# Seeding the scores' bank with the mask: a ScalarE copy in place of a TensorE product, in a six-layer decoder stack

## The reference

```
q = l2norm(q) * qs
k = l2norm(k) * ksc
... rotary turn of q and k with scales
mask = (it < jb) | (it > jb + w) | (jb == -1)
sim = jnp.einsum('bhwie,bhwje->bhwij', bq, bk2) * QK_SCALE
sim = jnp.where(mask, -jnp.finfo(sim.dtype).max, sim)
attn = jax.nn.softmax(sim, -1)
out = jnp.einsum('bhwij,bhwje->bhwie', attn, bv2)
```

## Time and profile before

| | us |
|---|---|
| median of 3 runs | 1274.28 (1273.89 to 1277.31) |
| the profiled execution | 1272.33 |
| its span in the trace | 1270.5 |
| layers, first to last mask | 410.7 to 1220.7 |
| TensorE busy in the span | 1138.3 (90%) |
| VectorE busy | 949.0 (75%) |
| ScalarE busy | 847.5 (67%) |
| GpSimdE busy | 650.1 (51%) |

### The profile page before, as it was taken

One profiled execution on the slowest core, in us unless ns is written; L12 is line 12 of the kernel. 1 busy time (PEld: TensorE's weight loads), 2 busy tenths in 40 slices (PEclk: granted clock), 3 DMA queues, 4 the chain that ended last, 5 costly groups with the idle time before them and its releaser, 6 DMA issues. The chain is left out here.

```text
span 1270.5 us, 26317 instructions
## 1 busy us (share of the span) xinstructions
PE 1138.3 (90%) x9636; PEld 720.2 (57%) x9636; DVE 949.0 (75%) x1399; ACT 847.5 (67%) x1356; POOL 650.1 (51%) x522
## 2 busy tenths in 40 slices
PE   7787869999765899999999999999999999999976
PEld 2222337777422576666656676666666666667541
DVE  2789957777465778787878788877878787878733
ACT  4553536665335588777877788678877787777844
POOL 1555723444323675664657465655566465756510
PEclk9888979999786899999999999999999999999997
DMA  3000007110200454344525453435434453534310
GB/s 113 1 1 0 1 17 217 51 50 1 77 24 19 97 155 99 93 123 107 133 74 129 103 134 88 112 102 134 99 98 123 109 126 76 126 90 120 87 49 17
DMA packets 75510, 107.11 MB, mean 84 GB/s; under 512 B 25347, under 2 KB 31938, under 8 KB 75002
## 3 DMA queue, kind: packets, MB, share of 16 engines
q1 hardware_dynamic: 75386, 105.47, 31.9%
HBM read 30.89 MB, written 0.59 MB: 25 GB/s over the span
## 5 line engine op out<-in xcount | busy, mean ns | idle before, releaser
L1680 POOL TENSOR_TENSOR st_sq_sum<-h 128x512 f32<-128x512 f32 x96 | 123.5, 1287 | 250.0 <-ACT h L1426 249.4
L1563 DVE SCALAR_TENSOR_TENSOR st_turned<-banks,mo_w 128x1024 f32<-128x1024 f32 x96 | 117.6, 1225 | 74.6 <-ACT banks L1437 43.2
L1426 ACT ACTIVATE h<-banks 128x512 f32<-128x512 f32 x192 | 112.1, 596 | 68.2 <-PE banks L1269 64.9
L1684 POOL TENSOR_TENSOR mo_w<-mo_w,x 128x512 f32<-128x512 f32 x96 | 122.5, 1276 | 61.4 <-DVE x L1549 60.5
L1330 PEld LDWEIGHTS banks<-st_p_blocks,st_vs 128*64 128x64 f32 x1536 | 81.8, 138 | 78.6 <-issue 74.6
L1289 PEld LDWEIGHTS banks<-st_wv,stream 128*128 128x128 f32 x768 | 100.6, 191 | 45.4 <-issue 44.7
L1686 POOL TENSOR_TENSOR mo_w<-mo_w,x 128x512 f32<-128x512 f32 x96 | 122.4, 1275 | 0.0
L1277 PE MATMUL banks<-st_sq_sum,head_ones 128*128 128x512 f32 x192 | 103.3, 620 | 16.1 <-POOL st_sq_sum L1680 16.1
L1458 ACT ACTIVATE st_p_blocks<-banks 64x512 f32<-64x512 f32 x192 | 112.2, 584 | 3.2 <-PE banks L1318 0.8
L430 POOL TENSOR_TENSOR ma_dbx<-ma_u,ma_b_rows 128x1024 f32<-128x1024 f32 x32 | 75.4, 2360 | 75.8 <-ACT ma_b_rows L288 51.9
L1693 POOL TENSOR_TENSOR mo_w<-st_prob,st_ri 128x512 f32<-128x512 f32 x96 | 100.2, 1044 | 15.2 <-DVE st_ri L1651 15.2
(11 more groups left out here) (234 smaller groups left out, 2780.1 us busy)
## 6 DMA issues: line engine op xcount, KB each, us to landing
st_qT<-st_turned SPq DMA_DIRECT2D x192, 128.0 KB, 2.4
st_k_blocks<-st_turned SPq DMA_DIRECT2D x384, 64.0 KB, 2.0
st_vs<-st_vn SPq DMA_DIRECT2D x96, 192.0 KB, 2.5
st_w_raw<-in_w_qk SPq DMA_DIRECT2D x12, 512.0 KB, 4.7
st_vs<-st_vn SPq DMA_DIRECT2D x96, 48.0 KB, 2.1
mo_w_all<-gate_rows SPq DMA_DIRECT2D x1, 3072.0 KB, 12.9
st_wv<-in_w_v SPq DMA_DIRECT2D x12, 256.0 KB, 3.0
st_wo<-in_wo SPq DMA_DIRECT2D x12, 256.0 KB, 3.0
```

The costliest lines, as they stand in the source:

```text
L1426: A(sq[:, part, :], ps[:, part, :], ACT.Square).then_inc(sq_done.sem, 1)
L1563: v.scalar_tensor_tensor(turned[:, h % 4], NORM_BANK.unsqueeze(1).to_broadcast([P, 2, SEQ]), 1e12, cos_part[:, which], ALU.min, ALU.mult). ...
L1680: nc.gpsimd.tensor_tensor(sq_sum[:], sq[:, 0, :], sq[:, 1, :], ALU.add).then_inc(sq_summed.sem, 1)
L1684: nc.gpsimd.tensor_tensor(cos_part[:, which, 0, :], cos_part[:, which, 0, :], sin_part[:, 1, :], ALU.subtract).then_inc(add_done.sem, 1)
```

## The change

The product of identity and mask is run once, ahead of the six layers, and increments a new semaphore `bits_set`. For each unit ScalarE now copies the mask from SBUF into the bank, as a step of its own queue between `copy_probs` and `copy_v`, after the same wait for `sub_done`, and increments `mask_done`, for which `scores` waits on TensorE. The products of `scores` are as before: they add into what stands in the bank.

```
-        def masks(s, n):
-            if sub_done.any(s.turn, n):
-                pe.wait_ge(*sub_done.at(s.turn, n))
-            mm(SCORE_BANK, C["ident16"], C["mask16"], start=True, stop=False, skip_group_check=True)
         def scores(s, n):
             pe.wait_ge(*heads_in[r][pair].at(s.turn, HEADS_IN * (g // 2) + HEADS_IN))
+            pe.wait_ge(*mask_done.at(s.turn, n + 1))
...
-                if t >= -2 and s.unit(t + 2):
-                    masks(s, t + 2)
...
+        mm(SCORE_BANK, C["ident16"], C["mask16"], start=True, stop=False, skip_group_check=True).then_inc(bits_set.sem, 1)
         pe.wait_ge(pads_zero.sem, 3)
         all_turns(pe, body)
...
+        def mask(s, n):
+            if sub_done.any(s.turn, n):
+                ac.wait_ge(*sub_done.at(s.turn, n))
+            A(SCORE_BANK, C["mask16"], ACT.Copy).then_inc(mask_done.sem, 1)
...
                 if s.unit(t) and t >= 0:
                     copy_probs(s, t)
+                if t >= -2 and s.unit(t + 2):
+                    mask(s, t + 2)
...
         ac.wait_ge(pads_zero.sem, 3)
+        ac.wait_ge(bits_set.sem, 1)
         all_turns(ac, body)
```

More of the change, by code:

```diff
@@ L1145, in build_stack @@
     pt_copied = flow("pt_copied", 2 * UNITS)
+    mask_done, bits_set = flow("mask_done", UNITS), flow("bits_set", 0)
     wo_step = flow("wo_step", UNITS)
```

## The result

| | before | after |
|---|---|---|
| median, us | 1274.09 (1267.60 to 1277.31, 10 runs) | 1288.10 (1282.27 to 1292.64, 10 runs) |
| the profiled execution | 1272.33 | 1291.54 |
| its span | 1270.5 | 1289.7 |

The ratio is 1.0113, 95% interval 1.0090 to 1.0136: about 14 us slower. The direction and the range held; the forecast was 9 us. The profiled execution of after is 3.4 us over the median of its ten. Of the 19.2 us between the two profiled executions, 2.3 lie ahead of the first scores (415.0 in the trace of before, 417.4 after), where the change adds one product. From the first scores to the last are 808.1 us before and 825.0 after, 16.9 more.

A forecast was written before the change was run, and what follows sets the result against it. TensorE's queue, waits for ScalarE's queue or another chain bound different steps. Profiled 1272.33 + 12.5 (copies) − 3.4 (products) = 1281.4, or 1283.4 us on the median, 0.7% slower; forecast bounds 1281.5 to 1292, stated range 1276 to 1292.

The forecast's parts named there:

- The twelve waits of the earlier trace: Once per job, TensorE's variance product L1348 waits for ScalarE's square of the centred rows, 15.0 us in all.
- At t=1, 3 and 11: Steps where GpSimdE's sum of squares comes last, by 17 head norm waits (16.1 us), so removing the product gains nothing.
- The gain on TensorE: Removed mask products give back 0.21 us (bounds 0.11, 0.22) in 16 steps at t=2, 9, 10: 3.4 us.
- The copy's price: Each mask copy costs ScalarE's queue 0.52 us, bounds 0.49 and 0.69, and no idle.
- another distance to the next start than 0.5: Sign of being wrong: a mask copy on ScalarE whose start lies other than 0.5 us before the next start.
- Two copies per job: Two mask copies delay the square in each of twelve jobs: 24 x 0.52 = 12.5 us lost.
- L1340 follows copy_out there too: Before t=8, after t=4 to 7, the projection follows copy_out, so the previous step's copy, 0.52 us, also delays the job.
- 10.44 to 11.4 at t=8: Sign of being right: the step where a feed-forward job begins grows by about a microsecond.
- values' copy, logarithm, root, the square of the centred rows and copy_out: Listed as what is queued behind the mask's copy on ScalarE, which costs 0.52 us.
- costs nothing: At t=5 to 7 ScalarE's slack of 0.54 us takes up the copy's 0.52, the step staying about 6.94.
- faster: Rival: TensorE is the bound and ScalarE has room; 96 x 0.21 = 20 us gained, 1254 us; chance 0.10.
- taken up: Rival: the lateness at job starts is absorbed, so no change, 1274 to 1280 us; chance 0.17.

The follow-up runs named there:

- e2: The kernel before with no mask at all, neither product nor copy, so masking is left out: 0.9954 of the kernel before.
- e5: The changed kernel with the mask's copy moved behind the square of the centred rows at each job's first step alone: 1.0050 of the kernel before.
- e6: The kernel before with the mask put by ScalarE's copy only at t=2, 9 and 10, by TensorE's product elsewhere: 0.9972 of the kernel before.
- e1: The changed kernel with a product of the same size left on TensorE ahead of the head norm: 1.0128 of the kernel before.
- e9: The changed kernel with feed-forward weights issued at t=6, plus six products filling TensorE's wait for the square: 1.0057 of the kernel before.
- e4: The changed kernel with the five feed-forward weight transfers issued at t=6 instead of t=5, behind the keys: 1.0072 of the kernel before.
- e7: The kernel before with the five feed-forward weight transfers issued at t=6 instead of t=5: 0.9984 of the kernel before.
- e3: The changed kernel with the mask's copy behind the values' copy instead of ahead of it: 1.0087 of the kernel before.

## Why the prediction was right, and where it was short

**The views.** The twelve waits of the earlier trace rows were the right place to look; the mean shares of the earlier trace rows would have given the opposite sign. *Shown* (e2, e5). But the forecast put "At t=1, 3 and 11" down to the 17 waits of the earlier trace rows, and that holds for two of the three: eleven of the 17 waits lie at t=3 and t=11, the others before and in the first turn, none at the t=1 of later turns, which keeps its 8.99 in e2 all the same; there the sum ends 0.05 before the head norm, too little to be listed as a wait.

**The gain on TensorE**, 16 x 0.21 = 3.4. Measured 5 x 0.21 + 6 x 0.22 + 5 x 0.10 = 2.9, and 3.6 by the ratio of e6. At t=9 the product's removal gave 0.10. The forecast took t=9 for "its like" of t=2 without a row of its own, and it isn't: the sum of squares ends 0.26 us before the head norm there, at t=2 0.63. Before, then after, TensorE with its loads of weights (PEld):

```profile
773.15 0.40 PEld L1277 LDWEIGHTS banks<-st_sq_sum,head_ones 128*128 128x128 f32 x2
773.35 1.02 PE L1277 MATMUL banks<-st_sq_sum,head_ones 128*128 128x512 f32 x2
...
780.97 1.27 POOL L1685 TENSOR_TENSOR st_sq_sum<-h 128x512 f32<-128x512 f32 x1 [2.52 <-ACT h L1423]
782.29 0.30 PEld L1278 LDWEIGHTS banks<-st_sq_sum,head_ones 128*128 128x128 f32 x2
782.29 1.13 PE L1278 MATMUL banks<-st_sq_sum,head_ones 128*128 128x512 f32 x2
```

Counted from the start of the scores (768.45, 777.60) the head norm comes 0.21 sooner, 0.05 behind the sum. But its load of weights, which began 0.20 ahead of it under the mask's product, now begins with it, and the head norm takes 1.13 in place of 1.02. That is the case the forecast had as its lower bound, 0.11, and dropped. *Shown* (e1, e2, e6). The Trainium skill's 216 ns for a lone product of 512 columns (TensorE: Matmul & The Clock Gate, Back-to-back issue gap) fits the 0.21 and 0.22; its 131 for a stream doesn't.

**The copy's price**, 0.52 with bounds 0.49 and 0.69. Measured 0.49 in the wait of L1346, at the lower bound. The whole duration, 582 ns, isn't what the queue pays. The forecast's sign for being wrong, "another distance to the next start than 0.5", did come, 0.61, and it misled: the price is 0.49 all the same, since the copies ahead give way sooner. The Trainium skill (ScalarE: Activation LUTs, Step-by-step: what each stage is for) calls a bank the faster destination of ScalarE; the medians here, 582 ns into the bank against copy_out's 579 out of one into SBUF, and 692 ns (L1437, into a bank) against 687 (L1433, into SBUF), don't bear it out.

**Two copies per job, 24 x 0.52 = 12.5.** At t=0 both are there, 0.97. At t=8 only one is in full: the forecast had it that "L1340 follows copy_out there too", but in the earlier trace rows it starts without a wait. In e9 it waits 0.23 for copy_out there, and the rest of the second copy is at t=5, as 0.31 before the head norm (a wait for the sum of squares, 0.25 to 0.27), with 0.09 and 0.07 back at t=6 and t=7: 0.84 us over t=5 to 8 in the middle turns of e9, for 1.04 forecast. The sign "10.44 to 11.4 at t=8" didn't come, 10.9 did. The count was wrong too: the last turn issues no mask at its last two steps, so its second job loses neither copy; the twelfth wait of L1346 is 1.44 as before, and 22 copies are left. In e9 all steps t=0 of turns 1 to 5 add 4.8 us, and t=5 to 8 add 3.4, since a wait for the keys in turns 0 and 3 of the kernel before (0.41 and 0.30) is gone there too: 8.2 us, 8.9 without that.

**The step that failed** is the list of what is queued behind the copy: "values' copy, logarithm, root, the square of the centred rows and copy_out". It stopped at ScalarE's own list and put the transfers at nothing. The values' copy has a queue waiting for it, SyncE's, in which the keys' transfers stand behind the values', and at t=5 five transfers of weights in between. That the copy "costs nothing" at t=5 to 7 was read from ScalarE's slack of 0.54 alone, and t=6 came out 7.21 to 8.76. About 5 us by the ratios of after and e4, part of which is the two low stretches of the clock behind waits for keys, and part of which the kernel before may have too (e7). *Shown* that the queue does it (e3, e4); the size is uncertain by some 4 us.

**The clock** is in no term: a longer wait was priced by its length. It took about 1.6 us more, 13 times in 44. About 2 us in the mean by the ratios of e4 and e9, whose intervals overlap, 3 to 8 in single traces (two such steps in e4, five in e1). *Shown in the traces* that it happens (13 of 44 against none of 77, and none in e9); its mean size is not shown.

Sum: 8.9 − 2.9 = 6.0 for the two engines (e9 measures 1.0057, 5.6 to 9.0 us by its interval); about 2 for the clock, about 5 for the queue: 13 to 14, against 14.0 between the medians. The last two are themselves differences of measured ratios (after to e4, e4 to e9), so that the sum closes is no check of them; the check is the 6.0 from the steps against e9's interval. That the result lies in the range is luck in part. The two terms that the forecast priced, +12.5 and −3.4, came to +8.9 and −2.9, that is +6.0: less than its lower bound of +7.4. The other 7 to 8 us came from the transfers and the clock, which it had at nothing. Of the rivals, faster fell with the waits for the square growing by the copy's 0.49, and "taken up" with t=0 at +0.97; at t=8, though, its first half, that L1340 waits for little there, was right.

## What to carry to other kernels

Before moving work to an engine with room, list who waits for each instruction behind the new place, on every queue and on the transfers' too, and follow each until the next wait; an issue queue at 0.6 us a transfer is an engine like the others. Where two engines bound different steps, choose the place step by step: the same copy is worth 0.1 to 0.2 us in three steps of sixteen and costs 0.5 in others. A wait that grows a little can cost more than its growth if TensorE's clock falls behind it.

## What was not expected of the hardware

The granted clock fell to its lower level for a stretch after 13 of 44 waits of 1.72 or 1.75 us and after none of 77 of 1.23 us, in the same place of the program; it fell after two of seven waits of 1.6 to 2.0 us elsewhere. What decides in the single case wasn't found. ScalarE's write of 128x512 bf16 from SBUF into a bank took 582 ns, about as long as copy_out's 579 out of a bank, and cost the queue 0.49; I had expected it between the 0.53 of the exponential and the 692 ns of the root.
